# Evoformer pair block on one core: weight loads moved, and the triangle layers' banks, biases, gates and table loads reordered

## The chip, the cores and the metric

The kernel runs on one core of a Trainium2 chip. The metric is device microseconds of one execution. Before the change the median of three runs is 271.05 us (270.81 to 274.38). A separately profiled execution, from which all rows come, took 270.19 us, of which 268.4 us are the profiled span.

## What is computed

The input is `z`, 64 x 64 positions of 32 channels in fp32. Six layers follow one another, each needing the whole result of the one before: two triangle multiplications, two triangle attentions (the second on the transposed grid), a two-layer transition, and an involution (a 5 x 5 filter generated at each position). The change touches the two triangle multiplications and the start of the first attention:

```python
def _tri_mul(z, ..., outgoing):
    x = _ln(z, lnw, lnb)
    a = sigmoid(x @ agw + agb) * (x @ apw + apb)
    b = sigmoid(x @ bgw + bgb) * (x @ bpw + bpb)
    t = einsum('bikc,bjkc->bijc' if outgoing else 'bkic,bkjc->bijc', a, b)
    t = _ln(t, lnow, lnob) @ zw + zb
    return t * sigmoid(x @ gw + gb)
z = z + tm(z, 0, True)
z = z + tm(z, 1, False)
z = z + ta(z, 0)      # attention: q.k scores + bias, softmax, values, gate
```

## The kernel before, in words

**Layout.** The grid is held as 128 partitions (4 row groups x 32 channels) by 1024 columns (16 rows x 64 positions), in two halves of 512 columns, so one half fills one PSUM bank. There are eight banks, `bank[0]` to `bank[7]`.

**Order.** Nothing schedules the program: each engine has its own list of instructions, written out in order (`@block.tensor`, `@block.scalar`, `@block.vector`, `@block.gpsimd`, `@block.sync`), with semaphores between them. `pe.wait_ge(sig(name), at(name, n))` holds everything that is behind it on that engine.

**One triangle layer on TensorE** (names `tm0`, `tm1`): a layer norm is a centring product (L827), squares on ScalarE (L433), a mean product (L838), logarithm and exponential on ScalarE (L438, L444), and two VectorE operations for `x` (L603, L606). Then the operands `a` and `b` are made in two halves `hb`: four bias products (L868) and 64 small projections (L883) per half, followed on ScalarE by four tanh (L475) and on VectorE by four products into `ab` (L661). The output gate has its own projection (L891) and tanh (L483). `triangle` (L902) multiplies `ab` with itself, 32 products; its result leaves PSUM through `tP` (L492 on ScalarE, L669 on VectorE), is transposed back (L927), copied (L498, L676), normed (`lno`), projected (L935) and added as `upd` (L693). In `tm0` a second layer norm, `lng`, of the transposed input feeds the gate; its centring stands between the projections and the triangle. In `tm1` the gate is re-laid out: GpSimd permutes it (L361), SP writes it to a DRAM tensor (L315), reads it back in four pieces (L318), and GpSimd settles it into `gateR` (L370), which `upd` needs.

**Keeping TensorE occupied.** `keep_warm(b, n)` (L819) issues n products of 128 x 256 whose results nobody reads. An fp32 product of the source is two instructions on TensorE, so n products count 2n in the rows.

**Loads.** SP issues all loads of inputs, first the image and the first weights, then `cst`, `tmw` (second half), `ptw`, `taw`, `ivw1`, `qk`, and last the involution weights `ivw2` (1600 KB, read from a tensor `inv_w`). The query-key products (`query_key_products`, L858) combine the query and key weights; VectorE scales them into `wyh` (L624), which the first attention's L979 uses. They need nothing of the image. `w2s` (L641) is a 3200-column VectorE operation on the involution weights.

**Tables.** `nc.scalar.preload_act_table_set` loads the function table that ScalarE needs for Ln or Tanh.

Of the kernel before, what the change touches and what calls it, by code (L numbers as in the profile page):

```python
# [19 lines left out]
ACT = mybir.ActivationFunctionType  # L20
# [4 lines left out]
N = 64  # L25
C = 32
GB = 128 // C
# [4 lines left out]
H = 4  # L32
# [29 lines left out]
def build_program(nc, z_rows, z_cols, vecs, consts, selrow, tm_w, tm_rows, ta_w, ta_qk, pt_w, inv_w1, inv_w2, out):  # L62
    with ExitStack() as ctx:
# [157 lines left out]
        AB_BANKS = ((4, 5, 6, 7), (2, 3, 4, 5))  # L221
# [47 lines left out]
        def kern_banks(i):  # L269
# [5 lines left out]
        WARM_START, WARM_LN, WARM_WEIGHTS = 3, 5, 4  # L275
        WARM_KERNEL = 4
# [4 lines left out]
            "tm0_lng": (z0T, xg, 1, (0, 1), (2, 3), "tm0_lnin", "eps5"),  # L281
            "tm0_lno": (tB, y, 0, (6, 7), (4, 5), "tm0_lnout", "eps5x16"),
            "tm1_ln": (upd, x, 0, (0, 1), (2, 3), "tm1_lnin", "eps5"),
            "tm1_lno": (tB, y, 0, (6, 7), (4, 5), "tm1_lnout", "eps5x16"),
# [12 lines left out]
        def _(sp):  # L297
# [130 lines left out]
        def _(act):  # L428
# [22 lines left out]
            def layer_norm(name, then_tanh=True):  # L451
                nc.scalar.preload_act_table_set("natural_log_exp_and_others")
# [26 lines left out]
            def gate_tanh(st, s, chs=(0, 1)):  # L479
                for ch in chs:  # L480
                    act.wait_ge(sig(f"{st}_gproj"), at(f"{st}_gproj", ch + 1))
                    act.wait_ge(sig("halfgb"), at("halfgb", 1))
                    nc.scalar.activation(half(th, ch), bank[(2, 0)[s] + ch], ACT.Tanh, bias=halfgb[:, s:s + 1],  # L483
                                         scale=0.5).then_inc(sig(f"{st}_gtanh"), 1)

            def t_out(st):
                for b in (0, 1):
                    act.wait_ge(sig(f"{st}_t"), at(f"{st}_t", T_ORDER.index(b) + 1))
                    if st == "tm0" and b == 1:
# [3 lines left out]
                                         bank[4 + b][0:64, :].rearrange("m (c g n) -> m c g n", c=8, g=GB),  # L493
                                         ACT.Copy).then_inc(sig(f"{st}_tP_act"), 1)

            def t_back(st):
                act.wait_ge(sig(f"{st}_ttr"), at(f"{st}_ttr", 1))
                nc.scalar.activation(sorted_cols(half(tB, 0)), raw_cols(bank[2][:, :]), ACT.Copy).then_inc(sig(f"{st}_tB_act"), 1)  # L498
# [9 lines left out]
            layer_norm("tm0_lno")  # L508
# [3 lines left out]
            gate_tanh("tm1", 1, (0,))  # L512
            ab_tanh("tm1", 1)
            gate_tanh("tm1", 1, (1,))
            t_out("tm1")
            t_back("tm1")
            layer_norm("tm1_lno", False)

            def attention(st, s):
                layer_norm(f"{st}_ln")  # L520
# [71 lines left out]
        def _(dve):  # L592
# [28 lines left out]
            def score_weights():  # L621
                for s in range(2):
                    dve.wait_ge(sig("qk_product"), at("qk_product", s + 1))
                    nc.vector.tensor_tensor(wyh[:, s * 512:(s + 1) * 512].rearrange("p (h m) -> p h m", h=H),  # L624
                                            bank[s][:, :].rearrange("p (h m) -> p h m", h=H),
# [12 lines left out]
            def other_weights():  # L638
                score_weights()
# [26 lines left out]
            def tm_rest(st, s, g, zres, znew, others, weights):  # L666
                for b in (2, 3):
                    dve.wait_ge(sig(f"{st}_t"), at(f"{st}_t", T_ORDER.index(b) + 1))
                    nc.vector.tensor_copy(tP[:, :].rearrange("m (n g c) -> m c g n", g=GB, c=C)[:, 8 * b:8 * b + 8],  # L669
                                          bank[4 + b][0:64, :].rearrange("m (c g n) -> m c g n", c=8, g=GB)).then_inc(sig(f"{st}_tP_dve"), 1)  # L670
                if st == "tm0":
                    dve.wait_ge(sig("bias_products"), 1)
                    nc.vector.tensor_tensor(folded[:, :], bank[3][:, 0:3], vec[:, VEC["fold_tm0"]:VEC["fold_tm0"] + 3],
                                            ALU.add).then_inc(sig("folded"), 1)
                dve.wait_ge(sig(f"{st}_ttr"), at(f"{st}_ttr", 2))
                nc.vector.tensor_copy(sorted_cols(half(tB, 1)), raw_cols(bank[3][:, :])).then_inc(sig(f"{st}_tB_dve"), 1)  # L676
# [28 lines left out]
            def attention(st, s, zres, znew, others, part_of):  # L705
                layer_norm(f"{st}_ln")

# [104 lines left out]
        def _(pe):  # L812
# [27 lines left out]
            def layer_norm(name, waits, warm=None):  # L840
# [5 lines left out]
                keep_warm(2 if name.endswith("lno") else 4, warm)  # L846
# [5 lines left out]
            def query_key_products():  # L852

                pe.wait_ge(sig("in_qk"), at("in_qk", 16))
                for s in range(2):
                    for h in range(H):
                        q0 = s * 1024 + h * 128
                        last = mm(bank[s][:, h * 128:(h + 1) * 128], qk[:, q0:q0 + 128], qk[:, q0 + 512:q0 + 640], start=True, stop=True)  # L858
# [34 lines left out]
            def triangle(st, lhs_kind, between):  # L893

                pe.wait_ge(sig(f"{st}_ab"), at(f"{st}_ab", 8))
                for c in [hf * CH + cc for cc in range(CH) for hf in range(2)]:
# [5 lines left out]
                    last = mm(bank[4 + c // 8][0:64, (c % 8) * N:(c % 8 + 1) * N].rearrange("p (g r) -> p g r", g=GB),  # L902
# [4 lines left out]
            def triangle_back(st, s, in_gap):  # L907
                if st == "tm0":
# [4 lines left out]
                    for tm in range(2):  # L913
                        mm(bank[3][:, tm:tm + 1], tmw[:, tm * 768 + 640:tm * 768 + 768], V(f"tm{tm}_lnout_b"), start=True, stop=True,
                           skip_group_check=True)
                    mm(bank[3][:, 2:3], ptw[0:C, 0:128], V("pt_b")[0:C, :], start=True, stop=True,
                       skip_group_check=True).then_inc(sig("bias_products"), 1)
                    keep_warm(2, 1)
# [335 lines left out]
```

## Time and profile before

| | |
|---|---|
| median of 3 runs | 271.05 us (270.81 to 274.38) |
| profiled execution | 270.19 us |
| its span | 268.4 us |
| instructions | 6438, of them 2738 products and 2738 weight loads on TensorE |
| mean granted TensorE clock | 0.947 of full |
| HBM read / written | 6.59 MB / 2.23 MB |

The engines are PE (TensorE products), PEld (its weight loads), DVE (VectorE), ACT (ScalarE), POOL (GpSimd) and SP. An engine name with a q stands for its sequencer. In the chain of waits, "issue" is time in which the engine waited for nothing that the profile shows. A granted clock of 1.00 is 2.4 GHz, 0.50 is 1.2 GHz. By stage, from the timeline: the first triangle layer runs to 46 us (its transposes L927 start at 33.3 us, its `upd` L693 at 45.4 us), the second to 76 us, the two attentions to about 212 us, transition and involution to the end.

### The profile page before, as it was taken

Reading aid. Unit: us, or ns where it says so; the run is one execution under the profiler, and the core shown is the slowest. Engines: PE = TensorE matmul, PEld = TensorE weight load, DVE = VectorE, ACT = ScalarE, POOL = GpSimd, SP = SyncE. Lnnn points to the kernel's source line nnn. Section 1 sums busy time; section 2 is a strip of 40 time slices with the busy share of each in tenths; the row PEclk is TensorE's granted clock in tenths of the full one; section 3 lists DMA queues with packets and bytes.
Section 4 is the critical chain, followed back from the end, with each engine's and each line's share of the span. In section 5 each row is a group of like instructions: output and inputs, shape, how many; then the busy total and the mean of one; then the engine's idle time right before and its main releaser. Section 6 shows DMA issues by size and latency. Waiting matters only on the chain.

```text
span 268.4 us, 6438 instructions
## 1 busy us (share of the span) xinstructions
PE 237.8 (89%) x2738; PEld 130.1 (48%) x2738; DVE 144.6 (54%) x238; ACT 129.7 (48%) x227; POOL 107.5 (40%) x108
## 2 busy tenths in 40 slices
PE   8949799998999896999769998799986998899993
PEld 4635554558444543655433453356653534355541
DVE  0513275534884657566510356657662245999970
ACT  3717458744856448565652736766665632000001
POOL 5000000204430135977750003497887000598891
PEclk9956869999999999999975999999999999999999
DMA  6850000132305000000000010000000000000002
GB/s 232 262 218 2 2 0 0 79 83 81 78 1 166 22 0 2 2 2 4 2 4 0 9 23 0 2 4 2 2 2 4 0 0 18 0 0 0 0 2 78
DMA packets 5820, 9.34 MB, mean 35 GB/s; under 512 B 1952, under 2 KB 4064, under 8 KB 5632
## 3 DMA queue, kind: packets, MB, share of 16 engines
q1 hardware_dynamic: 5312, 8.76, 10.0%
q8 instruction: 22, 0.36, 0.6%
q10 hardware_dynamic: 288, 0.16, 0.2%
q14 instruction: 6, 0.05, 0.1%
q0 software_dynamic: 192, 0.00, 0.0%
HBM read 6.59 MB, written 2.23 MB: 33 GB/s over the span
## 4 chain that ended last, share of the span: by engine, by line
PE 61%; POOL 16%; issue 9%; ACT 7%; DVE 4%; POOLq 1%; ACTq 0%; DVEq 0%
POOL lnroom L424 10%; PE psum L827 8%; PE psum L838 6%; PE psum L819 6%; PE psum L979 5%; PE psum L1009 4%; PE psum L1059 3%; POOL soft L396 3%; PE psum L902 3%; PE psum L1003 3%; PE psum L883 3%; POOL og L410 3%; PE psum L1100 3%; PE psum L1079 2%; PE psum L1046 2%
## 5 line engine op out<-in xcount | busy, mean ns | idle before, releaser
L396 POOL TENSOR_TENSOR soft<-soft,rinv 128x512 f32<-128x512 f32 x32 | 33.3, 1042 | 19.3 <-DVE rinv L752 18.4
L739 DVE TENSOR_REDUCE mx<-psum 128x8 fp32r<-128x512 f32 x32 | 21.4, 672 | 19.1 <-PE psum L1009 19.1
L553 ACT ACTIVATE soft<-psum 128x512 f32<-128x512 f32 x32 | 19.1, 598 | 18.4 <-PE psum L1059 18.4
L1146 PE MATMUL psum<-lnroom,cst 128*128 128x512 f32 x48 | 22.9, 599 | 1.2 <-POOL lnroom L424 1.2
L1059 PE MATMUL psum<-cst,soft 128*128 128x128 f32 x128 | 20.9, 286 | 2.9 <-POOL soft L396 1.2
L749 DVE TENSOR_REDUCE rsum<-soft 128x8 f32<-128x512 f32 x32 | 21.6, 674 | 3.5 <-ACT soft L547 3.5
L387 POOL TENSOR_SCALAR gth<-gth 128x512 f32<-128x512 f32 x16 | 9.5, 619 | 33.2 <-ACT gth L540 33.2
L410 POOL TENSOR_TENSOR og<-gth,y 128x256 f32<-128x256 f32 x30 | 21.7, 728 | 2.5 <-ACT y L559 2.5
L547 ACT ACTIVATE soft<-psum 128x512 f32<-128x512 f32 x32 | 19.1, 596 | 5.0 <-PE psum L1064 5.0
L1059 PEld LDWEIGHTS psum<-cst,soft 128*128 128x128 f32 x128 | 13.4, 140 | 13.7 <-ACT soft L553 7.8
L588 ACT ACTIVATE Y<-psum 128x512 f32<-128x512 f32 x2 | 1.1, 594 | 38.8 <-PE psum L1146 38.8
L1133 PE MATMUL psum<-zst,w2s 128*128 128x512 f32 x50 | 18.5, 486 | 1.1 <-DVE gth L805 1.0
L361 POOL COPY vals<-z1T 128x1024 f32<-128x1024 f32 x1 | 1.9, 1934 | 43.3 <-DVE z1T L697 43.3
L1079 PE MATMUL psum<-soft,vals 64*32 64x64 f32 x1024 | 15.1, 226 | 4.3 <-ACT y L559 3.7
L1009 PE MATMUL psum<-Y,x 32*64 32x256 f32 x256 | 17.5, 387 | 0.0
L424 POOL TENSOR_TENSOR lnroom<-gth 128x1024 f32<-128x1024 f32 x3 | 7.1, 2374 | 24.7 <-DVE gth L805 24.7
L805 DVE SCALAR_TENSOR_TENSOR gth<-psum,vec,soft 128x1024 f32<-128x1024 f32 x13 | 16.2, 1278 | 1.4 <-issue 0.7
L433 ACT ACTIVATE lnroom<-psum 128x512 f32<-128x512 f32 x14 | 8.4, 598 | 15.8 <-PE psum L827 15.8
L1079 PEld LDWEIGHTS psum<-soft,vals 64*32 64x32 f32 x1024 | 10.2, 108 | 11.6 <-issue 10.0
L805 DVE SCALAR_TENSOR_TENSOR vals<-psum,vec,soft 128x1024 f32<-128x1024 f32 x12 | 15.0, 1279 | 1.0 <-issue 0.7
L559 ACT ACTIVATE y<-psum 128x256 f32<-128x256 f32 x30 | 11.7, 389 | 7.7 <-POOL og L410 7.7
L819 PE MATMUL psum<-cst 128*128 128x256 f32 x60 | 15.0, 390 | 0.0
(143 smaller groups left out, 450.5 us busy)
## 6 DMA issues: line engine op xcount, KB each, us to landing
gth<-inv_w SPq DMA_DIRECT2D x1, 1600.0 KB, 9.6
hop<-vals SPq DMA_DIRECT2D x2, 512.0 KB, 2.8
vals<-hop SPq DMA_DIRECT2D x8, 128.0 KB, 3.0
tmw<-tm_w SPq DMA_DIRECT2D x2, 384.0 KB, 4.3
z0R<-z_rows SPq DMA_DIRECT2D x2, 256.0 KB, 3.3
z0T<-z_cols SPq DMA_DIRECT2D x1, 512.0 KB, 6.3
hop<-gate SPq DMA_DIRECT2D x1, 512.0 KB, 2.6
z1T<-hop SPq DMA_DIRECT2D x4, 128.0 KB, 3.0
```

What stands on the lines that cost most here:

```text
L396: pool.tensor_tensor(PN[u % 2][:, :].rearrange("p (a k) -> p a k", k=N), E_[u % NE][:, :].rearrange("p (a k) -> p a k", k=N), rinv[:, 8 * ...
L410: pool.tensor_tensor(og[:, pos], gth[:, pos], avout[u % 2], ALU.mult).then_inc(sig(f"{st}_og"), 1)
L424: pool.tensor_tensor(psums[i % NSUM], prod[SUMS[j][0] % NPROD], prod[SUMS[j][1] % NPROD], ALU.add).then_inc(sig("inv_sum"), 1)
L739: nc.vector.tensor_reduce(mx[:, 8 * t:8 * t + 8], bank[t % 4].rearrange("p (a k) -> p a k", k=N), AX_X, ALU.max, negate=True).then_inc(sig ...
L749: nc.vector.tensor_reduce(rsum[:, 8 * u:8 * u + 8], E_[u % NE].rearrange("p (a k) -> p a k", k=N), AX_X, ALU.add).then_inc(sig(f"{st}_sum" ...
L805: nc.vector.scalar_tensor_tensor(rows8(prod[i % NPROD]), rows8(kern_banks(i)), vec[:, VEC["b2"] + p:VEC["b2"] + p + 1], xpad_v[:, p % KS:p ...
L819: mm(bank[b][:, 0:256], operand[:, 0:128], operand[:, 0:256], start=True, stop=True, skip_group_check=True)
L827: mm(bank[cb[ch]], K("center"), half(src, ch), start=name not in LN_OF_SUM, stop=True, skip_group_check=True).then_inc(sig(f"{name}_center ...
L1009: last = mm(bank[t % 4][64 * i2:64 * i2 + 64, :].rearrange("p (h a k) -> p h a k", h=H, a=2)[:, :, a, :], x[C * g:C * g + C, r * N:(r + 1) ...
L1059: last = nc.tensor.transpose(bank[T_BANK][:, 128 * h:128 * h + 128], PN[u % 2][:, 128 * h:128 * h + 128], K("ident"))
L1079: last = mm(bank[AV_BANK + a][C * h:C * h + C, 64 * i2:64 * i2 + 64], vals[64 * a:64 * a + 64, v0 + C * h:v0 + C * h + C], PT[u % 2][64 * ...
L1146: last = mm(bank[ch], K("ident"), half(term, ch), start=(j == LAG), stop=(j == len(SUMS) + LAG - 1))
```

## The change

**Loads.** SP waits until all eight `ab` products of `tm0` are made before it issues `taw`, `ivw1`, `qk` and `ivw2`. The wait on `z0T` goes.

**Banks.** The second operand half uses banks 0 to 3 instead of 2 to 5, so its bias products no longer wait for products of the first half. The triangle writes banks 0 to 3, the transposes back banks 6 and 7, the norm of the result banks 2, 3, 6 and 7, `lng` banks 4 to 7.

**TensorE's list.** `WARM_WEIGHTS` is 2 instead of 4; after the `tm1` and `ta0` norms the five warm products go; in `tm1` two stand between the third and fourth bias product. Both gate projections of `tm1` stand behind the second half's projections. The query-key products move from behind the second triangle to behind the norm of `ta0`, and two warm products take their place. In `tm0` the centring of the old `z` moves ahead of the output projection.

**ScalarE and VectorE.** Two table loads move or go: none stands ahead of the squares of either `lno` or of `ta0`; in `tm1` one stands ahead of `t_out`. Both gate tanh of `tm1` follow the eight `ab` tanh. `score_weights` (L624) moves from ahead of `w2s` to behind the norm of `ta0`.

TensorE, first triangle layer, from the warm products to the first mean product of `lng`. Before:

```order
L819 MATMUL psum<-cst 128x256 x4
L868 MATMUL psum<-rows,selr 128x512 x4
L883 MATMUL psum<-tmw,x 64x64 x64
L868 MATMUL psum<-rows,selr 128x512 x4
L883 MATMUL psum<-tmw,x 64x64 x64
L827 MATMUL psum<-z0T,cst 128x512 x2
L902 MATMUL psum<-ab 64x64 x16
L838 MATMUL psum<-Y,cst 128x512 x2
```

After:

```order
L821 MATMUL psum<-cst 128x256 x2
L870 MATMUL psum<-rows,selr 128x512 x4
L885 MATMUL psum<-tmw,x 64x64 x64
L870 MATMUL psum<-rows,selr 128x512 x4
L885 MATMUL psum<-tmw,x 64x64 x64
L829 MATMUL psum<-z0T,cst 128x512 x2
L904 MATMUL psum<-ab 64x64 x16
L840 MATMUL psum<-Y,cst 128x512 x2
```

The order is the same; the warm products are two instead of four, and (not shown in the rows) the second row of L868 waits for no `ab` product.

TensorE, second triangle layer, from the mean product of the norm to the transposes. Before:

```order
L838 MATMUL psum<-lnroom,cst 128x512 x2
L819 MATMUL psum<-cst 128x256 x5
L868 MATMUL psum<-rows,selr 128x512 x4
L883 MATMUL psum<-tmw,x 64x64 x64
L891 MATMUL psum<-x,tmw 128x512
L868 MATMUL psum<-rows,selr 128x512 x4
L883 MATMUL psum<-tmw,x 64x64 x64
L891 MATMUL psum<-x,tmw 128x512
L902 MATMUL psum<-ab 64x64 x32
L858 MATMUL psum<-soft 128x128 x8
L927 MATMUL psum<-cst,og 128x64 x16
```

After:

```order
L840 MATMUL psum<-lnroom,cst 128x512 x2
L870 MATMUL psum<-rows,selr 128x512 x3
L821 MATMUL psum<-cst 128x256 x2
L870 MATMUL psum<-rows,selr 128x512
L885 MATMUL psum<-tmw,x 64x64 x64
L870 MATMUL psum<-rows,selr 128x512 x4
L885 MATMUL psum<-tmw,x 64x64 x64
L893 MATMUL psum<-x,tmw 128x512 x2
L904 MATMUL psum<-ab 64x64 x32
L821 MATMUL psum<-cst 128x256 x2
L928 MATMUL psum<-cst,og 128x64 x16
```

Three warm products fewer, and the two that are left stand behind three of the bias products; L891 (now L893) is behind both groups of projections; the query-key products L858 between triangle and transposes have given way to two warm products.

TensorE, start of the first attention, from the centring of `ta0` on. Before:

```order
L827 MATMUL psum<-og,cst 128x512 x2
L838 MATMUL psum<-lnroom,cst 128x512 x2
L819 MATMUL psum<-cst 128x256 x5
L973 MATMUL psum<-x,taw 16x512 x2
L979 MATMUL psum<-x,wyh 128x512 x8
```

After:

```order
L829 MATMUL psum<-og,cst 128x512 x2
L840 MATMUL psum<-lnroom,cst 128x512 x2
L860 MATMUL psum<-soft 128x128 x8
L978 MATMUL psum<-x,taw 16x512 x2
L985 MATMUL psum<-x,wyh 128x512 x8
```

The eight query-key products stand where five warm products stood. Their result is scaled on VectorE behind the norm (L625), ahead of the copies of what L985 makes.

The diff, shortened:

```diff
-        AB_BANKS = ((4, 5, 6, 7), (2, 3, 4, 5))
+        AB_BANKS = ((4, 5, 6, 7), (0, 1, 2, 3))
...
-        WARM_START, WARM_LN, WARM_WEIGHTS = 3, 5, 4
-        WARM_KERNEL = 4
+        WARM_START, WARM_LN, WARM_WEIGHTS = 3, 5, 2
+        WARM_TRIANGLE, WARM_KERNEL = 2, 4
...
-            "tm0_lng": (z0T, xg, 1, (0, 1), (2, 3), "tm0_lnin", "eps5"),
-            "tm0_lno": (tB, y, 0, (6, 7), (4, 5), "tm0_lnout", "eps5x16"),
+            "tm0_lng": (z0T, xg, 1, (4, 5), (6, 7), "tm0_lnin", "eps5"),
+            "tm0_lno": (tB, y, 0, (2, 3), (6, 7), "tm0_lnout", "eps5x16"),
...
+            sp.wait_ge(sig("tm0_ab"), at("tm0_ab", 8))
             sp.dma_start(taw[:, :], ta_w).then_inc(sig("in_taw"), 16)
             sp.dma_start(ivw1[:, :], inv_w1).then_inc(sig("in_ivw1"), 16)
-            sp.wait_ge(sig("in_z0T"), at("in_z0T", 16))
             sp.dma_start(qk[:, :], ta_qk).then_inc(sig("in_qk"), 16)
             sp.dma_start(ivw2raw, inv_w2).then_inc(sig("in_ivw2"), 16)
...
-            layer_norm("tm0_lno")
+            layer_norm("tm0_lno", loaded=True)
...
             ab_tanh("tm1", 0)
-            gate_tanh("tm1", 1, (0,))
             ab_tanh("tm1", 1)
-            gate_tanh("tm1", 1, (1,))
+            gate_tanh("tm1", 1)
+            nc.scalar.preload_act_table_set("natural_log_exp_and_others")
             t_out("tm1")
             t_back("tm1")
-            layer_norm("tm1_lno", False)
+            layer_norm("tm1_lno", False, loaded=True)
...
             def other_weights():
-                score_weights()
...
                 layer_norm(f"{st}_ln")
+                if s == 0:
+                    score_weights()
...
                 for g in range(GB):
                     b = AB_BANKS[hb][g]
-                    if hb == 1 and b >= 4:
-                        pe.wait_ge(sig(f"{st}_ab"), at(f"{st}_ab", b - 3))
+                    if s == 1 and hb == 0 and g == GB - 1:
+                        keep_warm(b, WARM_WEIGHTS)
...
-                    keep_warm(2, 1)
+                    keep_warm(6, 1)
                 else:
-                    pe.wait_ge(sig("tm1_gtanh"), at("tm1_gtanh", 2))
-                    query_key_products()
+                    keep_warm(6, WARM_TRIANGLE)
...
-            centre("tm0_lng", ([("in_z0T", 16)], []))
+            centre("tm0_lng", ([("in_z0T", 16), ("tm0_ab", 2)], []))
...
-            triangle_back("tm0", 0, lambda: gate_projection("tm0", 0, xg, "tm0_lng_x", 2))
-            centre_residual("tm1_ln", z0T)
-            layer_norm("tm1_ln", ([("tm0_upd", 1)], [("tm0_upd", 2)]))
+            def in_first_gap():
+                gate_projection("tm0", 0, xg, "tm0_lng_x", 4)
+                centre_residual("tm1_ln", z0T)
+            triangle_back("tm0", 0, in_first_gap)
+            layer_norm("tm1_ln", ([("tm0_upd", 1)], [("tm0_upd", 2)]), 0)
             ab_biases("tm1", 1, 0)
             ab_projections("tm1", 1, 0)
             pe.wait_ge(sig("tm1_ln_x"), at("tm1_ln_x", 2))
-            gate_projection("tm1", 1, x, "tm1_ln_x", 0, (0,))
             ab_biases("tm1", 1, 1)
             ab_projections("tm1", 1, 1)
-            gate_projection("tm1", 1, x, "tm1_ln_x", 0, (1,))
+            pe.wait_ge(sig("tm1_ab"), at("tm1_ab", 2))
+            gate_projection("tm1", 1, x, "tm1_ln_x", 4)
             triangle("tm1", 1, lambda: None)
...
-                layer_norm(f"{st}_ln", ln_waits)
+                layer_norm(f"{st}_ln", ln_waits, 0 if s == 0 else None)
+                if s == 0:
+                    query_key_products()
...
+                        pe.wait_ge(sig("wyh_ready"), at("wyh_ready", 2 if s == 1 or h == 3 else 1))
                         mm(bank[YBANKS[ch][h]], wyh[:, s * 512 + h * 128:s * 512 + (h + 1) * 128], half(x, ch),
```

## Rows read from the trace of the kernel before

**Rows 1.** page, part 4, the chain that ended last, by engine

```profile
PE 61%; POOL 16%; issue 9%; ACT 7%; DVE 4%; POOLq 1%; ACTq 0%; DVEq 0%
```

**Rows 2.** stretches: from:to, length, PE busy (instructions), granted clock, DMA share, GB/s

```profile
9.70:12.40 2.70, 2.65 (x133) 1.00 1.02 368
12.40:14.70 2.30, 2.08 (x65) 1.00 0.99 274
14.70:24.80 10.10, 6.34 (x115) 0.50 0.27 110
31.80:38.60 6.80, 6.80 (x24) 0.50 0.00 0
38.60:60.00 21.40, 21.24 (x305) 1.00 0.16 51
```

**Rows 3.** chain of waits in order of time: start us, us, what

```profile
15.23 3.76 issue
18.99 1.29 PE psum L883 x61
20.28 3.71 PE psum L827 x4
```

**Rows 4.** timeline, 9 to 22 us: start, us, engine, line, tiles, count [idle before]

```profile
9.69 1.19 PE L868 MATMUL psum<-rows,selr 4*128 4x512 f32 x4
...
10.94 1.58 PE L883 MATMUL psum<-tmw,x 32*64 32x64 f32 x128
...
21.62 0.75 DVE L661 SCALAR_TENSOR_TENSOR ab<-soft,psum 128x256 f32<-128x256 f32 x2 [0.18 <-ACT soft L475]
```

**Rows 5.** page, parts 3 and 6: code packets; landing of the last weights

```profile
q8 instruction: 22, 0.36, 0.6%
...
gth<-inv_w SPq DMA_DIRECT2D x1, 1600.0 KB, 9.6
```

**Rows 6.** DMA view, 16.4 to 16.6 us, code queue

```profile
q8 instruction: 1, 0.02, 34.6%
```

**Rows 7.** DMA view, 54.9 to 55.1 us, code queue

```profile
q8 instruction: 1, 0.02, 41.5%
```

**Rows 8.** timeline, 49 to 67 us, second triangle layer

```profile
49.84 2.32 PE L819 MATMUL psum<-cst 128*128 128x256 f32 x10
...
51.29 0.55 DVE L606 TENSOR_SCALAR x<-lnroom,vec 128x512 f32<-128x512 f32 x1
...
53.21 1.59 PE L883 MATMUL psum<-tmw,x 32*64 32x64 f32 x128
...
56.93 0.73 PE L883 MATMUL psum<-tmw,x 32*64 32x64 f32 x42
...
57.82 1.17 PE L883 MATMUL psum<-tmw,x 32*64 32x64 f32 x86 [0.16 <-issue]
...
61.13 3.77 PE L902 MATMUL psum<-ab 64*64 64x64 f32 x64 [1.09 <-DVE ab L661]
...
64.83 2.05 PE L858 MATMUL psum<-soft 32*128 32x128 f32 x16
...
64.97 1.03 DVE L669 COPY og<-psum 64x512 f32<-64x512 f32 x1 [0.73 <-PE psum L902]
...
66.80 1.21 PE L927 MATMUL psum<-cst,og 64*128 64x64 f32 x16
```

**Rows 9.** timeline, 68 to 91 us: scaling, gate, first attention

```profile
68.65 1.28 DVE L624 TENSOR_TENSOR wyh<-psum,cst 128x512 f32<-128x512 f32 x2
...
70.97 3.33 POOL L370 TENSOR_SCALAR gateR<-vals 128x1024 f32<-128x1024 f32 x1 [6.89 <-DMA vals<-hop]
...
84.06 7.13 PE L979 MATMUL psum<-x,wyh 128*128 128x512 f32 x16
```

**Rows 10.** chain of waits, 70 to 76 us

```profile
72.52 1.72 PE psum L832 x4
...
75.37 0.76 DVE og L693
```

More of the change, by code:

```diff
@@ L449, in deviations, with layer_norm @@
                     inverse_deviation(name, ch)
-            def layer_norm(name, then_tanh=True):
-                nc.scalar.preload_act_table_set("natural_log_exp_and_others")
+            def layer_norm(name, then_tanh=True, loaded=False):
+                if not loaded:
+                    nc.scalar.preload_act_table_set("natural_log_exp_and_others")
                 squares(name)
@@ L482, in gate_tanh @@
                     act.wait_ge(sig("halfgb"), at("halfgb", 1))
-                    nc.scalar.activation(half(th, ch), bank[(2, 0)[s] + ch], ACT.Tanh, bias=halfgb[:, s:s + 1],
+                    nc.scalar.activation(half(th, ch), bank[4 + ch], ACT.Tanh, bias=halfgb[:, s:s + 1],
                                          scale=0.5).then_inc(sig(f"{st}_gtanh"), 1)
@@ L497, in t_back @@
                 act.wait_ge(sig(f"{st}_ttr"), at(f"{st}_ttr", 1))
-                nc.scalar.activation(sorted_cols(half(tB, 0)), raw_cols(bank[2][:, :]), ACT.Copy).then_inc(sig(f"{st}_tB_act"), 1)
+                nc.scalar.activation(sorted_cols(half(tB, 0)), raw_cols(bank[6][:, :]), ACT.Copy).then_inc(sig(f"{st}_tB_act"), 1)
             ab_tanh("tm0", 0)
@@ L845, in layer_norm @@
                     warm = WARM_LN - 1 if name in LN_BIAS_FOLDED else WARM_LN
-                keep_warm(2 if name.endswith("lno") else 4, warm)
+                keep_warm(0 if name.endswith("lno") else 4, warm)
             pe.wait_ge(sig("blank"), at("blank", 1))
@@ L857, in query_key_products @@
                         q0 = s * 1024 + h * 128
-                        last = mm(bank[s][:, h * 128:(h + 1) * 128], qk[:, q0:q0 + 128], qk[:, q0 + 512:q0 + 640], start=True, stop=True)
+                        last = mm(bank[6 + s][:, h * 128:(h + 1) * 128], qk[:, q0:q0 + 128], qk[:, q0 + 512:q0 + 640], start=True, stop=True)
                     last.then_inc(sig("qk_product"), 1)
@@ L901, in triangle @@
                     moved = ab[64 * hf:64 * hf + 64, :].rearrange("p (r g k) -> p g r k", g=GB, k=C)
-                    last = mm(bank[4 + c // 8][0:64, (c % 8) * N:(c % 8 + 1) * N].rearrange("p (g r) -> p g r", g=GB),
+                    last = mm(bank[c // 8][0:64, (c % 8) * N:(c % 8 + 1) * N].rearrange("p (g r) -> p g r", g=GB),
                               kept[:, :, lhs_kind * CH + cc], moved[:, :, :, (1 - lhs_kind) * CH + cc], start=True, stop=True)
@@ L913, in triangle_back @@
                     for tm in range(2):
-                        mm(bank[3][:, tm:tm + 1], tmw[:, tm * 768 + 640:tm * 768 + 768], V(f"tm{tm}_lnout_b"), start=True, stop=True,
+                        mm(bank[7][:, tm:tm + 1], tmw[:, tm * 768 + 640:tm * 768 + 768], V(f"tm{tm}_lnout_b"), start=True, stop=True,
                            skip_group_check=True)
-                    mm(bank[3][:, 2:3], ptw[0:C, 0:128], V("pt_b")[0:C, :], start=True, stop=True,
+                    mm(bank[7][:, 2:3], ptw[0:C, 0:128], V("pt_b")[0:C, :], start=True, stop=True,
                        skip_group_check=True).then_inc(sig("bias_products"), 1)
-                    keep_warm(2, 1)
+                    keep_warm(6, 1)
                 else:
-                    pe.wait_ge(sig("tm1_gtanh"), at("tm1_gtanh", 2))
-                    query_key_products()
+                    keep_warm(6, WARM_TRIANGLE)
                 pe.wait_ge(sig(f"{st}_tP_act"), at(f"{st}_tP_act", 2))
@@ L926, in triangle_back @@
                         pe.wait_ge(sig("folded"), 1)
-                    last = nc.tensor.transpose(bank[2 + n // HB][:, (n % HB) * N:(n % HB + 1) * N],
+                    last = nc.tensor.transpose(bank[6 + n // HB][:, (n % HB) * N:(n % HB + 1) * N],
                                                tP[:, n * 128:(n + 1) * 128], K("ident")[0:64, 0:64])
```

16 lines of the change are left out of this document (8 added, 8 removed).

## The prediction

> **What bounds the kernel now.** I read the page first: TensorE carries 61% of the chain of waits [rows 1], so a saving counts only where TensorE is late. Then the chain in order of time. At 15.23 us TensorE stands for 3.76 us with the releaser "issue" [rows 3]. It stands in the middle of the second group of projections, L883: no semaphore is waited for between two of them. Third, the table by stretch: the DMA engines are full from 9.7 to 14.7 us (share 1.02 and 0.99), and the granted clock is 1.00 (2.4 GHz) up to 14.7 us and 0.50 (1.2 GHz) from there to 24.8 us [rows 2]. Fourth, the DMA view, to see what could be missing in the middle of straight code. The code queue moved 22 packets, 0.36 MB [rows 5]; with the 2738 products and 2738 weight loads of TensorE that is one packet of about 16 KB for 249 instructions. One such packet moves at 16.5 us [rows 6], and TensorE goes on at 18.99. The same pair stands later: a packet at 55.0 us [rows 7], and L883 goes on at 57.82 after a small stop [rows 8]. So I read the 3.76 us as code that comes late because its packet queues behind the weights, the last of which take 9.6 us from issue to landing [rows 5].
>
> The Trainium skill (Runtime: NRT & Kernel Launch, Instruction fetch mechanics) has blocks of 256 instructions, fetched ahead, at a cost that is "mostly hidden". The block size agrees with the 249; the 3.76 us do not agree with "hidden". By that rule the stop has another cause and would stay; this is rival 2.
>
> **1. First triangle layer: loads deferred, banks.** Nothing moves up to the first projections, 10.94 to 12.5 us [rows 4]; `rows` is what L868 waits for, so two warm products fewer (0.9 us) only empty time ahead of 9.69. The second biases run as four in 1.19 us (as the first four did [rows 4]) to 13.65; before, two ran, then two waited. Projections go on until the code block ends. Half of a block is products, about 128, so if the old edge is at product 63 of the second group, the edge before it was near product 68 of the first, at 10.94 + 68 x 0.0124 = 11.8 us. How long does a block take without the queue? In the second layer the stop at 57.66 is at product 42 [rows 8]; going back 125 products over 4 biases and 2 L891 reaches product 49 to 51 of L883's first group, 53.84 us; TensorE went on at 57.82, thus 4.0 us. So the new block is there at 15.8 us, not 18.99; TensorE has arrived at 14.5 and **1.3 us of the 3.76 remain**. The last 61 products take 1.2 us at half clock (the last 61 to 65 took 1.29 [rows 3]): 17.0.
>
> Then `lng` centring, 3.71 us at half clock [rows 3], ends at 20.7, and the triangle starts there instead of at 24.0 (20.28 + 3.71): gain **3.3 us** if the clock is low all that time. The other bound: at full clock the projections end at 16.6, the last `ab` product comes 2.1 us behind them (20.28 to 22.37 [rows 3, 4]), the triangle starts at 18.7: gain **5.3**. The clock fell before 15 us while TensorE was busy 2.08 of 2.30 us with L868 and L883 alone [rows 2]; the change leaves exactly this work and less warm work before it, so I take 3.5, near the low end. The triangle, L914, L916 and the transposes follow as before; the second half-clock stretch there, 31.8 to 38.6 us [rows 2], has the same sparse work before it and stays.
>
> SP's wait holds four loads until about 19 us. `ivw2`, issued last, is under way by 20.5 and lands by 20.5 + 9.6 = 30 us [rows 5]; its first reader on VectorE stands behind the transposes (33.3 us before, so 29.8 now) and behind five more operations. `taw` and `qk` are wanted from 75 us. Cost 0. Behind SP's wait stands only the relayout of `z1`, due near 44 us.
>
> In the gap of `tm0`, the centring of `z` (1.72 us) now stands ahead of the output projection. `upd` starts at 45.4 us behind the gate's table load, tanh and VectorE work; the projection's first half, 1.72 us later than before, would end at 45.3: 0, at most -0.1. The table load that goes ahead of `lno` lies beside the centring at half clock: 0.
>
> **2. Second triangle layer, front.** `x` is ready at 51.84 us (51.29 + 0.55); TensorE now waits for it behind ten warm instructions, 2.32 us from 49.84, and biases, and starts L883 at 53.21 [rows 8]. Three biases, four warm instructions (0.93) and one bias end at 51.97: 1.2 us earlier. But the block edge that is at product 50 now falls near 61 of the first group, 52.75 us, because 10 warm and 2 gate instructions before the next edge are gone and 4 added. The next block is there at 52.75 + 4.0 = 56.75, while TensorE, without an L891 between, is at its edge at 55.5. The second group ends at 57.65 instead of 58.97: gain 1.3, not 2.5. ScalarE and VectorE need 2.1 us more, to 59.75. Both gate projections now stand ahead of the triangle: 1.88 us at full clock, to 59.5, hidden; 3.71 us at half clock, to 61.4. The triangle starts at 61.13 now [rows 8]. Bounds **+1.4 and -0.3**. Between 51.7 and 57.65 TensorE has only L868, L883 and a stop, the mix in which the clock fell before; now L891 stands in its midst and the clock was 1.00 [rows 2]. I take +0.4.
>
> **3. Between triangle and transposes.** L858 takes 2.05 us from 64.83 to 66.88; `tP` is out at 66.00 (64.97 + 1.03), the transposes start at 66.80 [rows 8]. Four warm instructions, 0.93 us, end at 65.8. The transposes start at 66.05: **+0.75**. Behind them VectorE is rid of the 1.28 us of L624 ahead of `w2s` [rows 9], so `y` could come earlier; but the chain there runs over L832, 72.52 to 74.24, on TensorE, not over `y` [rows 10]: 0. The table load that goes lies beside the centring: 0. What is late next is the gate's relayout: settled at 74.30 (70.97 + 3.33 [rows 9]), `upd` at 75.37 [rows 10]. If the gate tanh comes up to 1 us later than 61.2, it settles at 75.3 while `upd` would be due at 75.4 - 1.15 = 74.2. But those 3.33 us lie beside `w2s` on VectorE, and with the later arrival they would lie behind it. I take 0, bound -1.0.
>
> **4. First attention.** The query-key products (2.05 us) stand where 2.32 us of warm products stood, while `x` is made: 0. VectorE scales them in 1.28 us behind `x`, to 84.3; L979 starts at 84.06 with the first half of `wyh` 0.6 us earlier, and VectorE's first copy of its results is wanted only two of its products (0.9 us each) later: 0. But without the warm products TensorE has only small products for 4.3 us, and L979 then needs 7.13 us at full clock [rows 9]. [...] Bounds +0.25 and -1.2, I take -0.3.
>
> **Sum:** 3.5 + 0.4 + 0.75 - 0.3 = 4.35 us, 270.19 - 4.3 = **265.9 us**. The profiled execution was 0.86 us under the median of 271.05. From 76 us on the order is unchanged and moves as a whole.
>
> **The rivals.** *Rival 1, the clock holds.* For it: in `tm1` the clock was full through two groups of L883 [rows 2, 8]. Then 5.3 + 1.4 + 0.75 + 0.25 = 7.7: 262.5 us. Chance 0.25. The Trainium skill (TensorE: Matmul & The Clock Gate, What's actually happening) lets the clock follow how busy TensorE has been; TensorE was 90% busy ahead of the fall, so busyness alone would keep the clock and speaks for this rival, and the row for the fall speaks against it. *Rival 2, the stop is not the loads' doing,* it comes at the block's edge anyway: then only the bias wait and parts 3 and 4 remain, 0.5 + 0.75 = 1.2: 269.0. Against it is the packet at 16.5 us amid a full DMA. Chance 0.08. *Rival 3, the front's gains are eaten:* the clock falls in `tm1` and `ta0`, or the gate's relayout comes last: 3.3 - 0.3 + 0.75 - 1.2 - 0.5 = 2.0: 268.2. Chance 0.14. *Rival 4, slower than before:* the clock stays low for long over full-size work. Half-clock stretches of 10.1 and 6.8 us are in the rows [rows 2]; over L827, L838, L891 and L979 each us of it costs 0.5. Against gains of 5.6 at full clock it decides from about 11 us of added half clock; two such stretches of 10 us, over the gate projections and norm of `tm1` and over L979, give 270.2 - 5.6 + 10 = 274.6. Against it: full-size products brought the clock back in every stretch. Chance 0.05. My forecast has 0.48: 264.6 to 267.3.
>
> **Range and chances.** 2% of 271.05, about what a measurement of this kernel can tell from no change, is 5.4 us: faster means below 265.6. From rival 1 0.25 and from the forecast's lower part 0.19: 0.44. Slower by 2% is the upper part of rival 4, 0.03. The range goes from 262.3, the clock holding, to 269.3, above rivals 2 and 3; outside are rival 4 and tails of rival 1.
>
> **What would show it.** At about 14.5 us a stop in L883 of 1 to 1.5 us with the releaser "issue", the triangle's start at 19 to 20.7, a DMA share near 1 only from about 19 us. A second stop of 1.2 us in `tm1`'s second group. A clock of 0.5 over the gate projections confirms part 2, one of 1.00 rival 1. The transposes of `tm1` 1.15 us behind the triangle's end, not 1.9. L979 in 7.1 us. If the stop at 14.5 is gone altogether or as long as before, step 1 is wrong.

## The result, and the profile after

The changed kernel takes 262.98 us (median of four, 262.68 to 263.23) against 270.96 us (four runs): the ratio is 0.9676, 95% interval 0.9599 to 0.9752, so it is faster by over 2%. The forecast was 265.9 us and, by its chances, a change within 2% as the likeliest outcome. Medians are over all executions of a kernel; ratios and their intervals leave out executions that were disturbed. The profiled execution took 262.68 us, with a span of 260.9 us and a mean granted clock of 0.961, which the other three had too, against 0.947 in the profiled execution of the kernel before.

The chain by engine (page, part 4), against [rows 1]:

```profile
PE 58%; POOL 17%; issue 8%; ACT 7%; DVE 6%; DMA 1%; POOLq 1%; ACTq 0%; DVEq 0%
```

The chain of waits of the first layer, against [rows 3] (start us, us, what):

```profile
14.57 0.35 issue
14.92 0.89 PE psum L885 x52
...
18.03 2.01 PE psum L904 x32
...
26.87 1.90 PE psum L928 x16
28.77 3.71 PE psum L829 x4
```

The chain counts only the products that are on it. The timeline counts all that the profile has, and shows that the stop stands behind product 67 of the second group:

```profile
13.64 0.93 PE L885 MATMUL psum<-tmw,x 32*64 32x64 f32 x67
```

The stop in the projections (L885 here) is down from 3.76 to 0.35 us. The triangle L904 starts at 18.03 us instead of 23.99, and at 26.87 the transposes still take 1.90 us, the centring L829 behind them 3.71: here the clock is at half.

By stretch, against [rows 2] (from:to, length, PE busy, granted clock, DMA share, GB/s):

```profile
12.50:14.60 2.10, 2.07 (x77) 1.00 0.03 8
26.90:33.60 6.70, 6.70 (x22) 0.52 0.00 0
50.90:54.10 3.20, 3.20 (x71) 0.53 0.19 55
54.30:91.00 36.70, 34.97 (x248) 1.00 0.21 64
```

The DMA engines, full in this place before, are at 0.03 while the projections run. The 10.1 us at half clock in the first layer are gone, the second stretch (6.7 us) has stayed, and a new one of 3.2 us lies over the gate projections of `tm1`.

The code packet, against [rows 6]: the DMA view of 12.5 to 12.7 us.

```profile
q8 instruction: 1, 0.02, 29.2%
```

The packet moves at 12.6 us, not at 16.5. The 1600 KB are issued at 19.24 us and land 8.4 us later, beside the triangle and what follows it.

The second layer, chain of waits, against [rows 8, 10]:

```profile
46.56 1.52 PE psum L885 x91
...
49.94 0.55 issue
50.49 1.52 PE psum L885 x70
52.01 2.86 PE psum L893 x4
54.87 3.75 PE psum L904 x64
...
59.81 0.69 PE psum L928 x8
...
68.12 0.76 DVE og L693
```

The second group stops behind product 53 (counted by the timeline) for 0.55 us; both gate projections take 2.86 us, partly at half clock; the triangle starts at 54.87. Two rows of the timeline, against [rows 9]:

```profile
64.92 1.16 POOL L370 TENSOR_SCALAR gateR<-vals 128x1024 f32<-128x1024 f32 x1 [6.44 <-DMA vals<-hop]
...
76.82 7.13 PE L985 MATMUL psum<-x,wyh 128*128 128x512 f32 x16
```

The gate settles in 1.16 instead of 3.33 us and is no bound, and L985 (before L979) needs its 7.13 us at full clock.

### The profile page after: what moved, and what is told of

Read it like the earlier page. It is cut to its first block, busy times and chain, and to the rows that moved or that the text cites. A ratio compares the mean times of both kernels' runs of the same rounds, so it can differ in the third digit from the quotient of the medians.

```text
span 260.9 us, 6408 instructions
## 1 busy us (share of the span) xinstructions
PE 233.7 (90%) x2722; PEld 126.9 (49%) x2722; DVE 145.1 (56%) x238; ACT 127.4 (49%) x225; POOL 105.4 (40%) x108
## 4 chain that ended last, share of the span: by engine, by line
PE 58%; POOL 17%; issue 8%; ACT 7%; DVE 6%; DMA 1%; POOLq 1%; ACTq 0%; DVEq 0%
POOL lnroom L424 10%; PE psum L829 7%; PE psum L840 6%; PE psum L985 5%; PE psum L1015 4%; PE psum L1065 3%; PE psum L904 3%; POOL soft L396 3%; PE psum L1009 3%; PE psum L821 3%; POOL og L410 3%; PE psum L885 3%; PE psum L1106 3%; PE psum L1085 3%; PE psum L1052 2%
## 5 line engine op out<-in xcount | busy, mean ns | idle before, releaser
L1152 PE MATMUL psum<-lnroom,cst 128*128 128x512 f32 x48 | 22.8, 598 | 1.2 <-POOL lnroom L424 1.2
L433 ACT ACTIVATE lnroom<-psum 128x512 f32<-128x512 f32 x14 | 8.4, 597 | 20.7 <-PE psum L829 20.7
L840 PE MATMUL psum<-lnroom,cst 128*128 128x512 f32 x28 | 14.6, 645 | 0.0
```

The costliest lines, as they stand in the source:

```text
L840: mm(bank[vb[ch]], K("mean"), half(sq[sset], ch), start=True, stop=True).then_inc(sig(f"{name}_var"), 1)
L1152: last = mm(bank[ch], K("ident"), half(term, ch), start=(j == LAG), stop=(j == len(SUMS) + LAG - 1))
```

## The experiments

Executions of one program on one chip differed in mean granted clock, and their time with it. So beside the ratios, executions of like mean clock are compared. This is a rough tool: e1 took 264.4, 264.6 and 266.61 us at a mean clock of 0.961, because it also counts where the clock is low.

**e1 and f1: the wait alone.** The kernel before, with only SP's wait added.

```diff
+            sp.wait_ge(sig("tm0_ab"), at("tm0_ab", 8))
             sp.dma_start(taw[:, :], ta_w).then_inc(sig("in_taw"), 16)
             sp.dma_start(ivw1[:, :], inv_w1).then_inc(sig("in_ivw1"), 16)
-            sp.wait_ge(sig("in_z0T"), at("in_z0T", 16))
```

> The kernel before with the change's SP wait alone: taw, ivw1, qk and ivw2 wait for the eight ab products of tm0; nothing else moves. Theory A (the long stop in L883 is code that queues behind these loads, and most of the gain comes from its end): the stop of 3.76 us at 15.2 us shrinks to 0.3 to 1.0 us, the first triangle starts 3 to 5 us earlier, and the time falls by 3.5 to 5.5 us, to 265.5 to 267.5 us. Theory B (the gain lies in banks, order and clock, the stop is only moved): the stop stays above 2.5 us and the time falls by less than 1.5 us. If the clock in the first projections depends on the stop, it stays 1.00 here up to the triangle; if it depends on the missing warm work, it falls near 14.7 us as before and the centring L827 takes 3.7 us.

Measured: 265.61 us, ratio 0.9788 (0.9675 to 0.99). The chain of waits of f1, the same kernel once more:

```profile
14.48 0.83 PE psum L883 x52
15.31 0.34 issue
15.65 0.92 PE psum L883 x54
...
18.80 2.01 PE psum L902 x32
```

The stop is 0.34 us and the triangle starts at 18.80 us (L883 ran until 16.57, as the chain passes on to ScalarE there). Theory A holds. In e1's own profile the stop is 0.01 us. On the clock both of the expected cases came: in f1 it held and the centring ran in 1.98 us, in e1 it fell at 17.4 us and L827 took 3.53.

**e2 and f2: the change without the wait.** The changed kernel, with the four loads issued early.

> The changed kernel with the four loads issued early again, as before the change. Theory A: a stop of 3 to 4 us comes back in the middle of the second group of L885, the triangle starts near 22 to 24 us instead of 18.0, and 3.5 to 5.5 us of the 8.0 us are lost: 266.5 to 268.5 us. Theory B: less than 1.5 us are lost, below 264.5 us. The second layer keeps its gain of 1.2 to 1.4 us in both.

Measured: 268.05 us, ratio 0.9863 (0.9745 to 0.9981). The chain of f2:

```profile
13.43 0.86 PE psum L885 x54
14.29 4.18 issue
18.47 1.25 PE psum L885 x58
19.73 3.54 PE psum L829 x4
23.26 1.94 PE psum L904 x32
```

The stop is back, with 4.18 us (3.37 in e2), at the product of L885's second group at which the changed kernel stops too (67). In f2 the code packet moves at 16.1 us, as late as before the change, with the DMA engines full (share 1.02 from 12.0 to 16.1 us). So the length of the stop comes from these loads; its place comes from the count of instructions, as e5 shows.

**e5: the block's edge moved.** 64 more instructions at the start.

```diff
             keep_warm(4, WARM_START, sq[0])
+            for _ in range(16):
+                mm(bank[4][:, 0:1], sq[0][:, 0:128], sq[0][:, 0:1], start=True, stop=True, skip_group_check=True)
```

> The changed kernel with 16 one-column products more at the very start, while TensorE waits for the image: 64 more instructions, under 1 us of work, in idle time. Theory A (code arrives in blocks of 256 instructions and a stop stands at a block's edge): every edge comes 32 recorded products earlier. In the first layer's second group of L885 the stop moves from product 67 to 35, in the second layer from 53 to 21, and both may change by a few tenths of a us. Rival (the stops come from the DMA or from TensorE's queue at a fixed time or a fixed place of the program): they stay at products 67 and 53. The time stays within 1.5 us of 263.0.

Measured: 269.75 us, ratio 1.0032 (0.9998 to 1.0066). The chain of waits:

```profile
4.12 6.62 PE psum L853 x32
...
21.90 0.55 PE psum L887 x35
22.45 0.14 issue
...
57.21 0.38 PE psum L887 x21
57.59 0.24 issue
```

The stops are behind product 35 and product 21, as forecast to the product: a stop stands at an edge that is set by a count of instructions, and 4 x 16 = 64 more moved it. The time was misjudged: the 16 added products cost 6.62 us, not under 1, all of it ahead of the image's centring. The centring and the mean product behind them were slow as well (3.62 and 2.91 us), and the first projections start at 19.25 instead of 10.98 us, 8.27 us later.

**a1: the changed kernel again.**

> The changed kernel once more, unchanged. Theory C (my sum for the first layer was 2.4 us short because the clock, whose fall there differs between executions of one program, held in that one execution): in this execution the clock may fall in the first projections, then the centring L829 takes 3.7 us and the triangle starts near 20.5 us instead of 18.0; the times spread by 2 to 5 us. Rival (the changed kernel holds the clock there by its order of work): the clock is 1.00 until behind the first triangle again, the triangle starts at 18.0 to 18.4 us, and all times lie within 0.5 us of 263.0.

Measured: 263.91 us (262.12 to 267.47), ratio 0.9813 (0.9754 to 0.9872). The chain of waits of its profiled execution, then two of its stretches (as above: length, PE busy, granted clock, DMA share, GB/s):

```profile
14.62 2.21 PE psum L885 x113
16.82 3.68 PE psum L829 x4
20.50 1.94 PE psum L904 x32
...
29.19 0.66 PE psum L928 x8
```

```profile
13.80:20.40 6.60, 6.60 (x134) 0.50 0.10 14
30.80:34.00 3.20, 3.20 (x4) 0.50 0.00 0
```

Theory C holds: here the clock was at half from about 13.6 to 20.3 us, the centring took 3.68 us and the triangle started at 20.50. That this is step 1's 20.7 is partly luck: TensorE was so slow that it did not stop for code at all. Behind the triangle the clock was full over the transposes (0.66 us for half of them) and fell at 30.6 us for 3.4 us, half as long as in the first profile; over the gate projections it held. From 10 to 60 us both executions have about 10 us at half clock; their mean clock is 0.961, and they take 263.16 (a1) and 262.68 us; the places differ.

**f3: the four kernels on one chip.**

> The changed kernel, again. Theory D: 262 to 263.2 us at a mean clock of 0.955 to 0.965, 5 to 6 us below the kernel before at the same clock; its executions at lower clock take 264 to 268. Rival: above 0.965 in most executions, so that like clocks are rare.

> The kernel before with the SP wait alone, again, to compare executions of like clock on one chip. Theory D (5.4 of the 8.0 us are the change's order of work, the rest is that the executions first compared had different clocks): at a mean granted clock of 0.955 to 0.965 this kernel takes 264 to 265.5 us, the one before 267 to 269. Rival (the change itself holds the clock, and that is part of its gain): even at like clock the four kernels differ by more than 6.5 us in all.

> The changed kernel with the loads issued early, again. Theory D: at a mean clock of 0.955 to 0.965 it takes 265 to 266.5 us, 3 us above the changed kernel, as much as the wait alone gains on the kernel before. Rival: 1.5 us or less, or over 4.5 us.

Measured, all on one chip with 17 executions of the kernel before (median 270.94):

| kernel | median, ratio (interval) | at a clock near 0.961 | at 0.967 or 0.968 |
|---|---|---|---|
| before | 270.94 | 0.959: 267.72; 0.962: 268.32 | 266.55 |
| f1, the wait alone | 265.63, 0.9885 (0.9821 to 0.9949) | 0.955: 265.94; 0.965: 264.46; 0.966: 265.33 | 264.79 |
| f2, the change without the wait | 266.43, 0.9912 (0.9868 to 0.9955) | 0.961: 265.8 to 266.18 (five) | 265.21 |
| f3, the change | 266.14, 0.9782 (0.9672 to 0.9891) | 0.961: 263.19 | 261.53 |

At like clock the change is worth 268.0 - 263.2 = 4.8 us here, and 5.5 on a1's chip (0.959 to 0.962: before 267.77 to 269.40, median 268.32; change 262.12, 262.78, 263.16). Near 0.967 it is worth 5.0, near 0.948 it is 3.8 (269.59 to 265.77). The wait alone gives 2.8 (268.0 to 265.2, the mean of the three), and taking it away from the change costs 265.9 - 263.2 = 2.7. This split is loose: at 0.967 or 0.968 the two are 1.8 and 3.7, and on e1's chip the wait alone gives about 4.4 (before at 0.962: 269.07 and 270.15; e1 at 0.961, mean 265.2). Theory D holds in the main: 3.8 to 5.5 of the first comparison's 8.0 us are wait and order together. Clock explains part of the rest: the first profile of before had 0.947, that of the change 0.961, and among f3's neighbours the kernel before took 268.0 at 0.96 and 269.59 at 0.949. f3's own executions went down to 0.921 (270.52 us), so the change does not hold the clock by itself. Its profiled execution took 265.77 us at a mean clock of 0.948:

```profile
14.23 0.72 issue
...
15.84 3.56 PE psum L829 x4
19.40 1.94 PE psum L904 x32
...
31.12 3.71 PE psum L829 x4
```

Here the clock is low in all three places that the forecast had: over the centring ahead of the triangle (16.0 to 19.4 us), behind the triangle (26.2 to 36.4), and over the gate projections (53.5 to 56.9). The time is almost the forecast's 265.9 us, though on another chip than the first comparison.

**e3: one gate projection between the projections.**

```diff
             ab_biases("tm1", 1, 1)
+            pe.wait_ge(sig("tm1_ab"), at("tm1_ab", 1))
+            gate_projection("tm1", 1, x, "tm1_ln_x", 4, (0,))
             ab_projections("tm1", 1, 1)
             pe.wait_ge(sig("tm1_ab"), at("tm1_ab", 2))
-            gate_projection("tm1", 1, x, "tm1_ln_x", 4)
+            gate_projection("tm1", 1, x, "tm1_ln_x", 4, (1,))
```

> The changed kernel with the first of the two gate projections of tm1 put back between the second biases and the second projections. Theory A with the clock: its 0.93 us lie beside the wait for the code block, so the stop of 0.55 us in the second group shrinks to 0 to 0.3 us, the clock holds at 1.00 through both groups, only one gate projection (0.94 us) stands behind them, and the second triangle starts 0.8 to 1.1 us earlier: 262.0 us. Rival (the stop does not depend on what stands ahead): the second group ends 0.9 us later and the time is 263 to 263.9 us.

Measured: 264.86 us in the median, 261.85 in the profiled execution, without an interval. The chain of waits:

```profile
48.85 1.05 PE psum L893 x2
49.91 1.53 PE psum L885 x91
...
53.57 3.82 PE psum L904 x64
```

The gate projection (L893) takes 1.05 us where TensorE would have waited for code; the second group runs without a stop, and the triangle starts at 53.57, 7.38 us after the first group's start (46.19), against 54.87 - 46.56 = 8.31 in the first profile of the change. But in a1, the same kernel with the clock at full here, it is 54.91 - 47.85 = 7.06 us with a stop of 0.51. So the 0.93 us are the half clock over the gate projections. Filling the stop gained nothing: work of 1.05 us stands in place of a stop of 0.51, and behind it TensorE waits for `ab` all the same (1.09 us in e3). That the order of e3 holds the clock is not shown. Its time at 0.961, 262.72 us, is no better than a1's 262.12 to 263.16.

**e4: warm products behind the first triangle.**

```diff
                 if st == "tm0":
+                    pe.wait_ge(sig("tm0_tP_act"), at("tm0_tP_act", 1))
+                    keep_warm(0, 3)
                     pe.wait_ge(sig("tm0_lng_logv"), at("tm0_lng_logv", 2))
```

> The changed kernel with three warm products (1.4 us at full clock) in TensorE's idle time behind the first triangle, 23.9 to 25.2 us. Theory (the half-clock stretch of 26.9 to 33.7 us comes from the sparse work ahead of it): the clock stays 1.00 there, transposes take 1.2 instead of 1.9 us and the centring L829 1.9 instead of 3.7; VectorE's chain then limits, and 1 to 2.5 us are saved: 260.5 to 262.0 us. Rival: TensorE's first-triangle products are themselves too sparse and the clock falls all the same: 263 us, or 0.2 us more.

Measured: 263.19 us (258.86 to 263.92), without an interval. The chain of waits of the profiled execution (263.31 us):

```profile
16.73 3.71 PE psum L829 x4
...
30.45 3.64 PE psum L829 x4
```

The expected gain did not come: the clock had fallen before the triangle in this execution, and fell once more over L829 (3.64 us) in spite of the warm products. a1 has the same two falls without them, and 263.16 us. One execution with a mean clock of 0.980 took 258.86 us; it was not profiled.

**e6: the query-key products back in the gap.** The products on banks 4 and 5 behind the second triangle, their scaling ahead of `w2s`.

> The changed kernel with the query-key products and their VectorE scaling back between the second triangle and its transposes; behind the norm of ta0 stands nothing in their place. If their move is worth what step 3 says, the transposes start 1.9 instead of 1.2 us behind the triangle's end and 0.6 to 0.9 us are lost: 263.7 us. Rival (TensorE waits there for the copies of the triangle anyway, and the move is worth nothing): 262.7 to 263.2 us.

Measured: 268.93 us (266.27 to 271.49), ratio 0.9978 (0.9931 to 1.0026), where a1 on the same chip has 0.9813: 4.5 us lost, not 0.7. The chain of waits:

```profile
61.22 1.98 PE psum L859 x16
63.19 1.74 PE psum L928 x16
64.93 3.71 PE psum L828 x4
68.64 2.56 PE psum L839 x4
...
74.35 0.76 DVE og L694
```

Its granted clock from 64 to 70 us:

```profile
64.00:70.00 6.00, 6.00 (x15) 0.50 0.36 86
```

From the products' start at 61.22, which is the triangle's end, to `upd` it takes 13.13 us; in the changed kernel 68.12 - 58.62 = 9.50. Of the 3.6 us, the order explains about the 0.7 of the forecast; the rest is half clock over L928, L828 (3.71 for 1.98) and L839 (2.56 for 1.82). None of ten executions has a clock above 0.955, while three of a1's six have 0.961. At a clock of 0.955 it took 266.27 and 266.90 us, the kernel before 268.88 and 269.83. The loss at like clock is between 0.6 us (0.942: 268.09 and 268.54 against 267.47) and 3 us (0.948 against 0.945: 267.7 and 264.67).

The other profiles settle more of this than e6 alone. Of the four profiled executions with the products in this gap, the clock fell behind the second triangle in three: e6 (63.4 to 70.2 us), e1 (61.8 to 72.0) and f1 (62.5 to 65.9). In the profile of before it held ([rows 8]: the transposes take 1.21 us). In none of the ten with warm products there instead did it fall. f1 has:

```profile
61.90 3.18 PE psum L827 x4
```

From the triangle's end to `upd` it takes 10.47 us before, 11.84 in f1, 14.19 in e1 and 13.13 in e6, against 9.50 in the changed kernel. So the order makes the fall likely and does not force it. Whether the missing warm products or the products in their place bring it is not separated.

**e7 and f4: a version from these.** e3's and e4's edits and two warm products in the first layer's stop.

```diff
             ab_biases("tm0", 0, 1)
+            pe.wait_ge(sig("tm0_ab"), at("tm0_ab", 1))
+            keep_warm(4, 2)
             ab_projections("tm0", 0, 1)
```

> The changed kernel with e3's and e4's edits and two warm products more between the second biases and the second projections of tm0, where TensorE waits for code. If sparse work is what lets the clock fall, it holds through both triangle layers: first triangle at 18.0 to 18.5 us in every execution, no half-clock stretch before 100 us, second triangle at 52 us, and 259 to 261 us. If the warm products only push work back, 263 to 264.5 us.

> The changed kernel with the gate projection between the projections, warm products behind the first triangle and in the first layer's stop, again. At a mean clock of 0.955 to 0.965 it takes 261 to 264.4 us, no less than the changed kernel by over 1 us; what it gains comes from executions at 0.97 to 0.98, with 258.5 to 261 us. Its median lies 0 to 3 us below the changed kernel's.

Measured: e7 264.21 us, ratio 0.9691 (0.9611 to 0.977), beside a1's 0.9813; f4 262.35 us, ratio 0.9703 (0.9593 to 0.9813), beside f3's 0.9782. The chain of waits of f4's profiled execution, at a mean clock of 0.942 and 267.35 us:

```profile
13.85 2.01 PE psum L821 x4
...
18.05 2.99 PE psum L829 x4
...
31.05 1.98 PE psum L829 x4
```

The clock fell in spite of the warm products (2.01 us for four instructions), so the forecast "in every execution" is wrong. Behind the triangle it held, and L829 took 1.98 us. In e7's profile (260.82 us) it was the other way round: the first triangle started at 17.98 us and the second at 52.72, near the forecast, but the clock fell at 28.3 us and L829 took 3.60. At a clock of 0.961 the version takes 264.06, 264.23 and 264.36 us, 1 us more than the change; why is not shown. Its executions at 0.974 to 0.987 took 258.15 to 261.01 us, and there are four such in twelve, against none in the change's sixteen. It beats the kernel before by about 3%. Against the change the intervals overlap; its median is 3.8 us below f3's and 0.3 us above a1's, so a lead is not shown.

## Why the prediction was right or wrong

The place of the gain was right, its size and therefore the outcome were not. Against the profiled execution the sum was 4.35 us and the result 7.5.

**Step 1, first layer: this is what failed.** Taken as 3.5, bounds 3.3 and 5.3; measured at the triangle's start 23.99 - 18.03 = 5.96, outside even the bound. It is 2.5 of the 3.15 us that the sum was short. Two parts of the term were mis-sized. The stop left over was 0.35 us and not 1.3: the time for a code block was taken as 4.0 us from the second layer, where the DMA share was 0.48 (53.84 to 57.82 us). In the changed kernel, from the edge near 11.87 (10.98 + 72 x 0.0124) to 14.92 it is 3.05 us at a share of 0.02, and about 3.2 us in the second layer at 0.36; so the transfers beside it are likely not the whole reason. And the centring was taken at half clock (+1.8 us), from the fall at 14.7 us in the trace of before. In this execution it ran in 1.99 us at full clock; in a1 it ran in 3.68 and the triangle started at 20.50, in f3 in 3.56 and at 19.40. I took one execution's clock for the program's. a1 and f3 show that it varies between executions of the same code.

**The second half-clock stretch of the first layer** was to stay: it did, with 6.7 us, in the first profile; in a1 it was 3.4 us, in f3 10.2. I laid both low stretches and a third one into one forecast. f3's profiled execution has all three and takes the forecast's time, 265.77 us at a mean clock of 0.948; the four executions of the first comparison, all at 0.961, do not. So the sum comes near an execution with about the clock that the profile of before had (0.947), in part because errors cancel: in f3 the triangle starts 4.6 us earlier than before and not 3.5, and the stretch behind it is 10.2 us long and not 6.8. How often an execution has that clock, the sum does not say.

**Step 2, front of the second layer.** Taken as +0.4. From `upd` of the first layer (45.40 and 39.58, 5.82 us gained) to the triangle (61.13 and 54.80, 6.33) it gained 0.51. Its parts came, some of another size: the stop at a new edge (0.55 us, forecast 1.2, again because a block took about 3.2 us and not 4.0), the second group's end 52.01 against 58.99, the half clock over the gate projections (2.86 us, forecast up to 3.7).

**Step 3.** Taken as 0.75; the transposes start 66.80 - 59.81 = 6.99 us earlier, 0.66 more than the triangle, and `upd` 7.25, 0.26 more again. The relayout was no bound. e6, e1 and f1 show what the step missed: with the products in the gap the clock fell there in three of four profiled executions, and the way to `upd` grew by 1.4 to 3.7 us over that of the kernel before. The step priced the move as work alone. In the execution from which all rows came the clock held, so this gain is not in the first comparison of profiles.

**Step 4.** Taken as -0.3: L985 starts 7.24 us earlier, and the clock held through it (row 54.30 of the stretches). It measured 0. No run shows the -0.3 or its bound of -1.2 us: in this profile and in those of a1, f3, e2 and f2 L985 takes 7.06 or 7.07 us on the chain. From there the distance grows from 7.24 to 7.5 us.

**The rivals.** Rival 1, the clock holds, gave 262.5 us and had 0.25; the result lies beside it, in part by luck, for the clock did not hold throughout: its 5.3 for the first layer was 5.96 by the triangle, and its 1.4 for the front of the second was 0.51. Rival 2 is refuted by e1, f1, e2 and f2: the stop at the first layer's edge is 0 to 0.72 us with the wait and 3.37 and 4.18 us without. The Trainium skill (Runtime: NRT & Kernel Launch, Instruction fetch mechanics) calls the cost of a block "mostly hidden"; the 0 to 0.72 us agree with it, the 3.37 and 4.18 us do not. The block of 256 instructions that the Trainium skill states there agrees with the 249 per packet, and e5 agrees with fixed blocks: 64 instructions moved both edges by 32 products. Rivals 3 and 4 did not come in the first comparison; the lowest clock seen for the change, 0.921, gave 270.52 us, between the two.

**The outcome.** At like clock the change gives 3.8 to 5.5 us, 1.4 to 2.1%, around the sum of 4.35. Of the 7.5 us between the first two profiled executions, 4.8 are the change near 0.961, and the step from 0.949 to 0.96 is worth 1.6 us in the kernel before on f3's chip; about 1 us stays unexplained. What sets the clock of an execution stays open, but for the gap behind the second triangle (e6). That the change made high clocks more frequent as a whole is not shown: medians over all executions are 8.5 us apart on a1's chip and 4.8 on f3's. The banks and the table loads had no run of their own. From the start of the first projections to the triangle f1 takes 7.60 us and the changed kernel 7.05, both at full clock and with a stop of 0.34 and 0.35 us, so the banks are worth about 0.55 us there.

## What to carry to other kernels

A stop in the middle of straight code, with no semaphore, a full DMA and a code packet moving late, was here code that queued behind bulk loads; try to hold back what is wanted late until the dense stretch of small instructions is fetched. Count instructions to find the next edge: work of another kind that is moved from between two dense groups takes away the cover of the next block, though filling a stop of 0.51 us with 1.05 us of work gained nothing (e3). And before pricing the granted clock from one trace, profile the same kernel twice: it is the term here that changed places between executions.

## What the runs showed that was not expected

- One recorded fp32 product of a single column took 207 ns with its weight load (e5: 6.62 us for 32); "small" products are not cheap. The centring behind them took 3.62 us, as it does at half clock, though the profile's rows give 1.00 there: its record of the clock begins with the first change, at 16.6 us.
- GpSimd's settle of 1024 columns takes 1.16 us almost alone and 3.33 us beside VectorE's `w2s` of 3.54 us [rows 9]: in the changed kernel it starts at 64.92, 0.25 us before `w2s` ends. Where it started in the midst of `w2s` (before, f1, e6), it ended 0.9 us after it, however early it started.
- Executions of one program on one chip spread by 9.6 us (before, f3's chip: 266.55 to 276.13), 11.3 us (a1's) and 12.7 us (e1's), roughly in step with a mean clock between 0.968 and 0.902.
